# GpSimd's bias addition behind VectorE's quantization, in the second layer of an AdaLN and LoRA feed-forward kernel

## The reference, cut to what matters

```python
x = x + L0_ffn(L0_cond(x, ...))      # per-sequence 64x64 mixing, then linear + top-2 of 8 LoRA experts
x = x + L1_ffn(L1_cond(x, ids))      # the second layer, which the change is in

# L1_cond: a linear layer with a bias and one of 32 LoRA adapters (rank 16) for each sequence
r = x @ base_weight.T + base_bias + (x @ A[id].T) @ B[id].T
# L1_ffn: both factors rounded to float8 (e4m3), product scaled, bias added
out = (fp8(r / s_in) @ fp8(w / s_w)) * (s_in * s_w) + bias2
```

## Time and profile before

| | |
|---|---|
| three runs | 2148.89, 2144.24, 2148.28 us; median 2148.28 |
| profiled execution, span | 2146.3 us (2.0 below the median of the runs) |
| TensorE busy / VectorE busy / GpSimd busy over the span | 94% / 79% / 26% |
| second layer | from about 1067 us to the end |
| TensorE's granted clock | 9 or more tenths in all 40 slices |

### The profile page before, as it was taken

One profiled execution on the slowest core, in us unless ns is written; L12 is line 12 of the kernel. 1 busy time (PEld: TensorE's weight loads), 2 busy tenths in 40 slices (PEclk: granted clock), 3 DMA queues, 4 the chain that ended last, 5 costly groups with the idle time before them and its releaser, 6 DMA issues.

```text
span 2146.3 us, 37287 instructions
## 1 busy us (share of the span) xinstructions
PE 2024.6 (94%) x11969; PEld 1896.7 (88%) x12032; DVE 1691.0 (79%) x4631; ACT 488.7 (23%) x1312; POOL 554.9 (26%) x470
## 2 busy tenths in 40 slices
PE   7989899999999999999999999999999999999997
PEld 6989899999999999999988788878887888888885
DVE  6898886555555555555579999999999999999999
ACT  3111111111111111111123322232223222322232
POOL 3644311111111111111123232233223332323222
PEclk9999999999999999999999999999999999999999
DMA  7754433233233332332444444444444444444442
GB/s 241 239 154 134 124 115 115 90 109 101 90 112 98 98 111 90 110 100 90 145 126 134 134 125 148 133 134 125 149 132 125 134 129 148 128 134 131 146 129 81
DMA packets 152577, 273.07 MB, mean 127 GB/s; under 512 B 30179, under 2 KB 101861, under 8 KB 152550
## 3 DMA queue, kind: packets, MB, share of 16 engines
q1 hardware_dynamic: 152550, 272.77, 41.6%
HBM read 163.62 MB, written 109.05 MB: 127 GB/s over the span
## 4 chain that ended last, share of the span: by engine, by line
PE 49%; DVE 43%; issue 5%; ACT 1%; SPq 1%; DMA 1%; DVEq 0%; ACTq 0%
PE bank_g L964 11%; PE bank_g L966 11%; PE bank_g L965 11%; DVE rounded L858 8%; DVE rqt L346 6%; PE bank_t L947 4%; DVE ht L327 4%; DVE obuf L888 3%; DVE val L856 3%; DVE rq_blocks L870 3%; DVE st_l L878 2%; PE bank_g L1018 2%; PE bank_g L1017 2%; PE bank_g L1016 2%; PE bank_f L1027 2%
## 5 line engine op out<-in xcount | busy, mean ns | idle before, releaser
L964 PE MATMUL bank_g<-w0h,st_h 128*128 128x384 f32 (+1 forms) x1536 | 524.9, 342 | 20.5 <-DVE x1buf L824 17.4
L966 PE MATMUL bank_g<-w0h,st_l 128*128 128x384 f32 (+1 forms) x1536 | 523.4, 341 | 0.0
L965 PE MATMUL bank_g<-w0l,st_h 128*128 128x384 f32 (+1 forms) x1536 | 523.1, 341 | 0.0
L1016 PE MATMUL bank_g<-w1h,st_h 128*128 128x352 f32 x1536 | 506.3, 330 | 2.9 <-DVE st_l L878 2.5
L1018 PE MATMUL bank_g<-w1h,st_l 128*128 128x352 f32 x1536 | 496.3, 323 | 0.0
L1017 PE MATMUL bank_g<-w1l,st_h 128*128 128x352 f32 x1536 | 496.1, 323 | 0.0
L553 POOL TENSOR_TENSOR xbuf<-xbuf,b_base_sb 128x1024 f32<-128x1024 f32 x64 | 153.7, 2402 | 707.0 <-PE bank_t L947 693.0
L964 PEld LDWEIGHTS bank_g<-w0h,st_h 128*128 128x128 f32 x1536 | 291.1, 190 | 23.8 <-DVE st_l L723 19.1
L1016 PEld LDWEIGHTS bank_g<-w1h,st_h 128*128 128x128 f32 x1536 | 289.1, 188 | 10.8 <-DVE st_l L878 3.5
L966 PEld LDWEIGHTS bank_g<-w0h,st_l 128*128 128x128 f32 x1536 | 291.2, 190 | 0.0
L965 PEld LDWEIGHTS bank_g<-w0l,st_h 128*128 128x128 f32 x1536 | 291.0, 189 | 0.0
(11 more groups left out here) (84 smaller groups left out, 2384.7 us busy)
## 6 DMA issues: line engine op xcount, KB each, us to landing
xbuf<-x SPq DMA_DIRECT2D x64, 512.0 KB, 4.0
x_scratch<-x1buf SPq DMA_DIRECT2D x64, 512.0 KB, 2.9
x1t_scratch<-x_blocks SPq DMA_DIRECT2D x256, 128.0 KB, 2.3
xbuf<-x1t_scratch SPq DMA_DIRECT2D x64, 512.0 KB, 3.7
x1buf<-x_scratch SPq DMA_DIRECT2D x64, 512.0 KB, 5.1
out<-obuf SPq DMA_DIRECT2D x64, 512.0 KB, 2.7
b_stack<-b_split SPq DMA_DIRECT2D x384, 64.0 KB, 3.3
raw<-a_split SPq DMA_DIRECT2D x128, 128.0 KB, 4.2
```

The source lines that it names most:

```text
L964: pe.matmul(to, st_h[:, rows], w0h[:, k, cols], start=(k == 0), stop=False)
L965: pe.matmul(to, st_h[:, rows], w0l[:, k, cols], start=False, stop=False)
L966: last = pe.matmul(to, st_l[:, rows], w0h[:, k, cols], start=False, stop=(k == KC - 1))
L1016: pe.matmul(to, st_h[:, rows], w1h_k[:, k, cols], start=(k == 0), stop=False)
```

## The change

GpSimd waits, ahead of the addition for tile t, for `rq_done` to reach t + 1, that is until VectorE has finished quantizing tile t. SyncE asks for plain x1 of tile t + 1 in its pass t, behind the wait for the addition of tile t - 1; before, it asked for that of tile t + 2 behind the addition of tile t. The load of turned x1 no longer waits for an addition. The new guard `more >= 1 and not first` leaves the load out in pass 0, since tile 1 is loaded ahead of the loop, and keeps it in pass 62.

```diff
                     if more == 2:
                         sp.wait_ge(lo_done[1], TILES + t + 1)
-                        sp.wait_ge(x1b_done, t + 1)
                         load_turned(t + 2, b)
-                        load_x1(t + 2, b)
+                    if more >= 1 and not first:
+
+                        sp.wait_ge(x1b_done, t)
+                        load_x1(t + 1, 1 - b)
...
                     if stored is not None:
                         pool.wait_ge(out_stored[b], stored)
+
+                    pool.wait_ge(rq_done, t + 1)
                     pool.tensor_tensor(obuf[:, b, :], x1buf[:, b, :], bias2_sb[:, :], ALU.add).then_inc(x1b_done, 1)
```

## The result

The changed kernel takes 2168.93 us (median of four runs, 2166.96 to 2171.08) against 2148.59 for the kernel before on the same chip; the ratio of the runs is 1.0097, 95% interval 1.0083 to 1.0112. It is slower by 20 us; 2161 was forecast, 2138 to 2180 the range.

A forecast was written before the change was run, and what follows sets the result against it. VectorE was taken as the bound, with a ring through `val` just as tight. Terms of -0.15, -0.10 and +0.47 us a pass over about 60 passes gave +13 us, so 2161 us, range 2138 to 2180.

The forecast's parts named there:

- The bound: VectorE's own list in the second layer, busy 904 of 944 us, 16.56 us a pass, was said to bound the kernel.
- First term: The addition's 2.07 us stall leaves L858, returns as waits for bank 0 and at cast L901: -0.15 us a pass.
- Second term: The adapter copies no longer run beside L878, which gets shorter: -0.10 us a pass.
- Third term: The adapter copies run beside L903 and the nine small casts L327: +0.47 us a pass, between 0 and 0.68.
- The sum: -0.15 - 0.10 + 0.47 = +0.22 us a pass on VectorE's list, about 60 passes, +13 us.
- (a): Rival: adapter data land later, so the copies run beside transpose L870, undisturbed; about 2141 us; chance 0.19.
- (b): Rival: small cast L901 need not wait for the addition, TensorE sets the pace at 15.42; 2080 us; chance 0.05.
- (c): Rival: the cast waiting for the addition also waits out the four copies, +1.2 us a pass; 2220 us; chance 0.04.
- What was called free: x1 loads, store, `finish` and `ht` cost nothing; last tile's addition holds up L346 instead of L863, saving below 1 us.
- The 0.4 to 0.6 us: By the shared-port rule alone, the addition's loss would shrink by the time L895 and L899 take.
- `val`: Ring from L888 through ffn, main and ScalarE's `val` to L851 and back to L888: two passes, 16.55 us each.

## Why the prediction was right

- **The bound.** VectorE's list with what GpSimd holds up in it was taken as the bound, and so it was: a change in which VectorE only stood still at other places moved the pass by what these places add up to. Its wait for bank 0 (83.3 us over 62 passes in the changed kernel) stayed under the addition as foretold. When the addition was halved, the pass fell by 0.80.
- **First term, -0.15 a pass.** Measured -0.08: L905 ends 7.71 into the pass on average, L901 ended at 7.79. GpSimd starts 0.14 to 0.16 behind the instruction that releases it, not 0.05; that row of before gave a release by TensorE. The experiment with the loads alone confirms that the place of the addition is worth next to nothing: 16.93 against 16.92. One reading of the earlier trace rows does not come out: the 3.08 of the addition is not its wait for L856 (0.84) and then 2.40, which is 3.24. No term uses it.
- **Second term, -0.10.** Measured -0.12 (L882 1.28 a pair against 1.40).
- **Third term, +0.47.** Right in kind, too small: (124.4 - 88.1) / 57 = +0.64, near the 0.68 that was its upper bound. The copies start at 8.7 on average, not 8.1. The store is asked for 0.9 before a pass begins and not 1.2 (1512.08 against 1512.99), and in the changed kernel plain x1 is asked for at +0.3 on average and not at -0.3. And still all four meet casts, because every one of them that holds up a cast pushes the row of casts on. The value should have been the rate (0.45 us per us of overlap) times the whole length of the copies, not the one case, in which VectorE got there when a third of them was over.
- **The sum.** -0.08 - 0.12 + 0.64 = +0.44, and -0.03 at L346; of this 0.355 arrive in the pass, the rest is more overlap between L882 and L855 (0.08 on average, where it was 0.03). The three terms were forecast with the right signs, and the size of the third is what the forecast is short by. 0.355 x 60 = 21 us, against 13.
- **Rivals.** (a), the copies beside the transpose, did not come by itself; made on purpose it gave 2146, where 2141 was said. (b) was out: L905 stood. (c) could not show itself here, since the copies were not queued yet when the addition ended (they start 1.0 later on average). The changed kernel with finish moved settles it: there the copies follow at once, and the cast still ends 0.04 after the addition (1516.52 against 1516.48).
- **What was called free.** The last addition was to hold up the copies L346 of the last tile. It did not, see the end.

The transpose kept its 1.25 and finish its 1.41 beside GpSimd in every run, and the casts and the copies of 256 columns did not keep theirs. That agrees with the rule of the Trainium skill (SBUF — State Buffer, section Who interferes with whom) that was weighed in the prediction: an instruction with at most one SBUF input and outside the two-port modes does not contend with GpSimd, while copies and casts can. The 0.4 to 0.6 us that the prediction drew from that rule alone were not won. The loss of the addition shrank by 0.08, because VectorE's wait for bank 0 (75.7 us in 57 passes, 1.33 each) lies under it as well, and that had to be read from the trace.

## What to carry to other kernels

A stall that two engines cause each other is not removed by moving it. Before an instruction is moved, write down beside each stretch of the other engine's list what it needs (here: transposes and PSUM readers nothing, casts, copies of 256 columns and instructions with two operands in SBUF everything), cut the work to the length of the free stretches, and look at what stands behind the moved instruction on its engine, since that moves as well. Loads that get issued earlier are not free either: their consumers start earlier, and they may start beside the wrong neighbour. And each time a stall is taken out, compute all the rings through the other engines again; here three of them (VectorE's list 16.5, finish to bank 0 16.0, `val` 16.1 to 16.5) lay within 1.2 us above TensorE's 15.43 (15.47 when it set the pace).

## What the runs showed of the hardware that was not expected

The last tile of the changed kernel, VectorE and GpSimd:

```profile
2153.83 2.88 DVE L346 COPY xbuf<-rq_blocks 32x160 bf16<-32x160 bf16 x12
...
2160.02 2.48 DVE L346 COPY xbuf<-rq_blocks 32x96 bf16<-32x96 bf16 x12
...
2153.08 2.34 POOL L611 TENSOR_TENSOR obuf<-x1buf,bias_sb 128x1024 f32<-128x1024 f32 x1 [11.19 <-DVE rq L867]
```

The twelve copies of 160 columns run beside 1.6 us of addition and take 2.88; the kernel before had 2.87 with no addition beside them. The copies of 256 columns are held up by an addition, 4.35 instead of 2.77. And 160 columns take as long as 256: 227 ns and 222 ns for one. A copy of 96 columns takes 194 ns, 33 less; if 256 columns went at that rate per column, one would take about 277 (an estimate). So the shorter ones, five and three blocks of 32 instead of eight, run in another way, slower for a column, and those of 160 without need of what GpSimd holds. The reason was not tried. Two things differ beside the size: the number of blocks is odd, and the destination is `xbuf` instead of `rqt`.
